# Eight of eleven routing pieces of the second batch behind the slots of the first expert phase, and no warm-up matmuls ahead of its first two phases

## What is computed

```python
h = tok(x, W, b);  h = concatenate([cls_tok, h], axis=1)
h = h + attn(layernorm(h))              # scores minus 0.2 x their 8 neighbours, softmax, values
# the part around the change, on x = layernorm(h), per token:
w_fk = topk_sparsify(softmax((x @ W_fk + b_fk) @ emb_fk_n.T), 4)   # 4 of 128 experts, first layer
w_rk = topk_sparsify(softmax((x @ W_rk + b_rk) @ emb_rk_n.T), 4)   # 4 of 128 experts, second layer
hid  = sum_n w_fk[n] * (x @ f_know[n])   # 192 -> 128
out  = h + sum_n w_rk[n] * (hid @ r_know[n])   # 128 -> 192
```

## Time and profile before

| What | Value |
|---|---|
| Time, median of 3 runs | 823.0 us (820.96 to 825.43) |
| Time of the profiled execution | 822.98 us |
| Its span | 821.3 us |
| Mean granted clock of TensorE | 0.856 |
| TensorE, matmuls | 615.0 us (75%) |
| VectorE | 378.1 us (46%) |
| ScalarE | 359.1 us (44%) |
| GpSimd | 400.6 us (49%) |
| Bytes moved by DMA | 147.13 MB, mean 179 GB/s |

### The profile page before, as it was taken

How to read it: one execution, slowest core, us unless ns; L and a number is a source line. 1 busy time by engine, 2 the same in 40 slices (tenths; PEclk the granted TensorE clock), 3 DMA queues, 4 the chain that set the end, 5 groups by cost and what they waited for, 6 DMA issues and landing times.

```text
span 821.3 us, 14397 instructions
## 1 busy us (share of the span) xinstructions
PE 615.0 (75%) x4572; PEld 517.9 (63%) x4572; DVE 378.1 (46%) x1337; ACT 359.1 (44%) x760; POOL 400.6 (49%) x397
## 2 busy tenths in 40 slices
PE   6798998989998874575999999988199804998000
PEld 5586876868787653343999889877187603676000
DVE  2846678879597999966930011110011110231132
ACT  4337285574757362234344434433047502576000
POOL 2433260523423056620773067774477773771674
PEclk9789999999998997655999999989599956999555
DMA  5253729476440675891577567799989724897432
GB/s 137 58 194 121 257 76 356 133 281 233 147 199 21 119 162 129 220 219 30 168 219 184 134 183 200 208 316 342 259 224 255 201 65 109 243 269 199 129 96 69
DMA packets 139574, 147.13 MB, mean 179 GB/s; under 512 B 12025, under 2 KB 123042, under 8 KB 139490
## 3 DMA queue, kind: packets, MB, share of 16 engines
q1 hardware_dynamic: 126114, 118.63, 50.2%
q0 software_dynamic: 13376, 27.41, 11.5%
HBM read 73.50 MB, written 72.50 MB: 178 GB/s over the span
## 4 chain that ended last, share of the span: by engine, by line
PE 41%; DVE 20%; POOL 11%; issue 11%; ACT 8%; DMA 6%; SPq 2%; POOLq 0%; DVEq 0%; ACTq 0%
PE bank L1231 19%; POOL gat L772 7%; PE bank L921 5%; PE bank L1219 5%; ACT qk_pad L1337 4%; POOL mid_dram L780 4%; DVE pick L2004 3%; PE bank L968 3%; DMA gat<-wide_dram,slots 2%; DMA wide_dram<-os_pair 2%; PE bank L1240 2%; DVE smax L1778 2%; PE bank L906 1%; DVE probs L1781 1%; PE bank L985 1%
## 5 line engine op out<-in xcount | busy, mean ns | idle before, releaser
L1231 PE MATMUL bank<-matrices,xsT 96*64 (+1 forms) x1632 | 224.6, 295 | 0.0
L1231 PEld LDWEIGHTS bank<-matrices,xsT 96*64 96x64 f32 (+1 forms) x1632 | 192.8, 139 | 23.1 <-issue 5.7
L772 POOL DMA_INDIRECT gat<-wide_dram,slots x152 | 145.9, 960 | 124.4 <-SPq L606 77.0
L757 POOL DMA_INDIRECT wide_dram<-x2b,slots x76 | 75.0, 987 | 84.0 <-issue 42.6
L2052 DVE TENSOR_SCALAR acc<-gat,wts 128x128 f32<-128x128 f32 x19 | 6.1, 319 | 231.7 <-DMA gat<-wide_dram,slots 231.7
L714 POOL TENSOR_TENSOR qk_sum<-qk_pad 64x888 f32<-64x888 f32 x16 | 26.8, 1676 | 155.5 <-ACT qk_pad L1337 139.0
L1548 ACT ACTIVATE os_pair<-bank 64x384 f32<-64x384 f32 x136 | 58.5, 478 | 72.3 <-DMA wide_dram<-os_pair 36.9
L780 POOL DMA_INDIRECT mid_dram<-comb,slots x76 | 74.0, 974 | 27.8 <-issue 21.6
L1561 ACT ACTIVATE xsT<-bank 96x512 f32<-96x512 f32 (+1 forms) x136 | 59.6, 487 | 58.2 <-PE bank L1219 56.8
L1542 ACT ACTIVATE os_pair<-bank 64x512 f32<-64x512 f32 x68 | 40.3, 592 | 85.3 <-PE bank L1231 79.1
L921 PE MATMUL bank<-tok_wT,pixT 128*128 128x192 f32 x384 | 70.6, 345 | 1.3 <-ACT pixT L1314 1.3
(11 more groups left out here) (196 smaller groups left out, 914.9 us busy)
## 6 DMA issues: line engine op xcount, KB each, us to landing
wide_dram<-zeros SPq DMA_DIRECT2D x6, 3328.0 KB, 14.0
mid_dram<-zeros SPq DMA_DIRECT2D x8, 1664.0 KB, 17.7
xs<-wide_dram SPq DMA_DIRECT2D x68, 192.0 KB, 3.1
wide_dram<-os_pair SPq DMA_DIRECT2D x68, 192.0 KB, 3.7
matrices<-in_L_ffn_f_know SPq DMA_DIRECT2D x8, 1536.0 KB, 15.2
matrices<-in_L_ffn_r_know SPq DMA_DIRECT2D x8, 1536.0 KB, 12.2
wide_dram<-os_pair SPq DMA_DIRECT2D x68, 128.0 KB, 2.8
xs<-mid_dram SPq DMA_DIRECT2D x68, 128.0 KB, 4.0
```

What stands on the lines that cost most here:

```text
L757: pool.indirect_dma_start(wide_dram[b], bass.IndirectOffsetOnAxis(ap=slots[:, t, e:e + 1], axis=0), x2b[:, t - BATCHES[b][0], :], None)\
L772: pool.indirect_dma_start(gat[i][:, e, :], None, wide_dram[b], bass.IndirectOffsetOnAxis(ap=slots[:, t, k:k + 1], axis=0))\
L1231: last = pe.matmul(out_bank[0:W, n * width:(n + 1) * width], xsT[r][0:kp, c:c + W], matrices[0:kp, bass.ds(starts[(r * SB + k) * 2 + half] ...
```

## The change

The pieces are renamed from `ahead` to `piece`. Pieces 0 to 2 stay ahead of phase 0; piece 3 + 4s + r follows, in phase 0, the products of slot r of step s on TensorE and its results on ScalarE, so that pieces 3 to 10 stand behind the eight slots of steps 0 and 1. `WARM` is 0 for phases 0 and 1 (24 and 20 before) and stays 24 and 16 for phases 2 and 3. Matrix chunk 7 is issued behind the loads of phase 0's first four slots instead of ahead of the waits for plan and scatters. The loads of the second layer's matrices are as they were: five in phase 1, six at its end. The whole diff:

```diff
--- before.py
+++ after.py
@@ -59,9 +59,9 @@
 DEPTH = (4, 3)
 PAIRS = RING // 2
 VALUE_BANK = (4, 6, 2, 5)
-WARM = (24, 20, 24, 16)
+WARM = (0, 0, 24, 16)
 SHARED = 3
-ROUTED = 11
+PIECES, ROUTED = 11, 3
 MIN_STEPS = -(-min(hi - lo for lo, hi in BATCHES) * ROWS * TOPK // (OWNED * W))
 assert MIN_STEPS > SHARED
 Y_BANK = (2, 4, 5, 6)
@@ -521,7 +521,7 @@
 
             sp.wait_ge(res_used, GROUPS + 1)
             sp.wait_ge(stored, 64 * GROUPS + 1)
-            load_f(range(6, EXPERTS // CHUNK))
+            load_f(range(6, 7))
 
             def load_rows(ph, s, r):
                 layer, b = PHASES[ph]
@@ -617,6 +617,7 @@
             sp.wait_ge(scattered[0], 64 * BATCHES[0][1])
             for r in range(RING):
                 load_rows(0, 0, r)
+            load_f(range(7, 8))
             expert_rows(0, rows_of_second)
             expert_end(0)
             sp.dma_start(x2b[:, 0:BATCHES[0][1], :], h2_tiles[:, 0:BATCHES[0][1], :]).then_inc(h2x_loaded, 16)
@@ -1166,7 +1167,7 @@
                 pe.matmul(bank[7][:, c:c + 256], x2T[t % 3][:, 0, :], r_mat[:, 0, :], start=True, stop=False)
                 return pe.matmul(bank[7][:, c:c + 256], x2T[t % 3][0:DH, 1, :], r_mat[0:DH, 1, :], start=False, stop=True)
 
-            def ahead(k):
+            def piece(k):
 
                 if k == 0:
                     ranks_after(t0)
@@ -1199,7 +1200,7 @@
                     plan(1, k - 8)
 
             for k in range(ROUTED):
-                ahead(k)
+                piece(k)
 
             def experts(ph):
 
@@ -1267,6 +1268,9 @@
                                     transposed(s + 1, r)
                         for r in (2 * q, 2 * q + 1):
                             products(s, r, starts)
+                            k = ROUTED + s * RING + r
+                            if ph == 0 and k < PIECES:
+                                piece(k)
 
                 each_step(pe, used, 0, step)
 
```

## The result

The changed kernel takes 813.5 us as the median of 4 runs (809.98 to 816.06), against 823.7 us for the kernel before on the same chip: ratio 0.9876, 95% interval 0.9827 to 0.9925, so 10 us (6 to 14) faster. Every ratio and interval in this document is taken from the undisturbed ("fast") runs alone, so where some runs of the kernel before were slow it is not the quotient of the two medians beside it. The profiled execution took 809.98 us, the quickest of the four; its span is 13.1 us under that of before. `<-issue` in the views is idle time in which the engine waited for nothing that the trace shows.

What follows compares the result with a forecast made beforehand. Bound: the chain of waits through TensorE's phases 0 and 1 to the batch 1 gathers at 581.01 us. Phase 1 starts 16.9 us earlier, less 3.0 us of low clock: 822.98 - 13.9 = 809 us, range 804 to 818 us.

Steps and rivals of the forecast that it cites:

- scatters as the next bound: Between phases 0 and 1: the last batch 1 scatter, at 454.6 us, sets the start of phase 1.
- 9 us of hand-over: Last batch 1 scatter to ScalarE's first copy of phase 1: 9.2 us, as between phases 2 and 3.
- first transposes of phase 0: TensorE's start of phase 0: 369.5 us in place of 395.60 us, including 2.34 us of value reads.
- low clock in phase 0, lost: Start of phase 0 without warm-up: 6.0 us of work at half speed, 3.0 us lost.
- waits up to piece 10: Phase 0: waits that the eight pieces add, 1.0 us in all, between nothing and 4 us.
- piece 10 ends: Last piece in phase 0: 369.5 + 25.9 of work + 1.0 of waits + 3.0 of low clock = 399.4 us.
- ScalarE's first copy of phase 1: Start of phase 1: 463.8 us in place of 480.67 us, 16.9 us earlier.
- what phase 1 takes more than before: Phase 1: 3.0 us lost to low clock at its start, after TensorE has been idle.
- The rival row: From 364.0 to 371.8 us TensorE is busy yet the clock stays at 0.50; cited for the late-clock rival.
- two clock rivals: Phase 0: clock up only near 391 us, 817 us, chance 0.10; or low until piece 10, 832 us, chance 0.08.
- chunk's cover: Phase 0: moved matrix chunk costs nothing, needed 28 us later at step 3, or over 30 us later by GpSimd.
- the gain is lost in phase 1: Rival: phase 1's matrix loads cost their stall again, 4 us idle and 3 us of clock; 816 us, chance 0.07.

Runs made afterwards that it cites:

- chunk7_back: Changed kernel with matrix chunk 7 issued ahead of the first rows of phase 0 again; 817.34 us, ratio 0.9947.
- moved_warm_kept: Changed kernel with the warm-ups of phases 0 and 1 kept (24 and 20 matmuls); 814.21 us, ratio 0.9907.
- warm_removed_only: Kernel before with only the warm-ups of phases 0 and 1 removed; 815.54 us, ratio 0.9897.
- half_scatter: Changed kernel with two of the four row scatters of each batch 1 tile left out; 799.34 us, ratio 0.97.
- after_again: The changed kernel itself, run again on a slower chip; 1030.06 us against 1050.66 us for the kernel before, ratio 0.9796.

## Why the prediction was right

The time lies in its range (804 to 818 us), with the sign as forecast, and the mechanism held up to and with the start of phase 1: pieces into phase 0, scatters as the next bound, 9 us of hand-over. 809 us was 4.5 us low against the median, and a gain of 13.9 us was forecast where 10.2 us were measured. By its steps, against the profiled execution:

| Step | Forecast | Measured |
|---|---|---|
| first transposes of phase 0 | 369.5 | 368.94 |
| wait for their rows | 0 | 0 |
| low clock in phase 0, lost | 3.0 us | 0.3 us |
| waits up to piece 10 | 1.0 us | 1.6 us |
| piece 10 ends | 399.4 | 397.27 |
| batch 1 scatters, first and last | 404.9, 454.6 | 402.76, 452.35 |
| TensorE ends phase 0 | 453.9 | 453.18 |
| ScalarE's first copy of phase 1 | 463.8 | 461.74 |
| what phase 1 takes more than before | 3.0 us | 7.3 us |
| gathers of batch 1 | 567.1 | 569.38 |

**The start.** The pieces end 1.7 us later than in the execution before (the last logits start at 366.16 where they did at 364.43 us), but the value reads' 2.34 us cost nothing: the transposes follow the rank matmuls at 368.94 us without a gap. My reading is that they ran beside matmuls that were already queued, where in the earlier trace rows TensorE had waited just before them; that is not shown, and between phases 0 and 1 the reads do leave 2.9 us idle behind 7.2 us of products. Two errors of the step so cancel, by luck: the 1.7 us are what executions differ by.

**The clock in phase 0.** It rose at 369.5 us, behind a stretch in which TensorE had worked without a gap from 365.7 us, through logits and ranks. The forecast had it at 374 to 377 us, and so it came in chunk7_back (377.3 us), behind a wait; that it came 5 us or more sooner here, worth 2.7 us, is luck. The rival row, 7.8 us of the same work at 0.50, is no rule either: with the same instructions the clock rose at 367.3, 369.5, 370.1 and 371.0 us in the traces of moved_warm_kept, the changed kernel, warm_removed_only and half_scatter, 3.4 to 3.8 us after TensorE began to work without a gap. The two clock rivals (817 and 832 us) are out. The rule of the Trainium skill that spoke for the slower one (TensorE: Matmul & The Clock Gate, "A second HAM failure mode: psum-queue depth-cycling") is not borne out here: through all eight pieces, with waits of 0.4 to 1.25 us, the granted clock stays 1.00 from 371 us on. Behind the 1.51 us wait of phase 1 it did fall, at 471.9 us.

**The waits.** 1.25 us for ScalarE, whose first copy starts at 370.76 us, 0.8 us behind its last exponential, and 0.39 us for the rows of step 1, which queued behind the moved chunk and took 9.4 us to land: 1.6 us. The 0.77 us of issue at 397.27 us lie behind piece 10 and delay only what TensorE does next. 25.9 + 0.3 + 1.6 = 27.8 us stand against the measured 28.3 us from 368.94 to 397.27 us; the slots and pieces themselves took 0.5 us more than forecast. The chunk's cover, 30 us by my count, was of the wrong user: what the chunk delays is the rows of step 1, which are needed 10 us later.

**The hand-over.** From the last scatter's start to ScalarE's first copy 9.4 us passed, where the phase 2 to 3 row gave 9.2 us. Half_scatter shows that the scatters set it.

**Phase 1** is the term of the sum that was mis-sized, 7.3 us for 3.0. From its first copy to the gathers it took 107.6 us, 100.3 before. At its start TensorE runs 10.7 us at low clock; from the first copy to the transposes of step 1 it takes 9.8 us in place of 5.5, of which 1.5 are the wait for rows behind the `x2b` reload. That wait and the work around it bring the clock down a second time (473.34 us: 4.64 us for 3.64), and the next pair takes 6.4 in place of 4.7 us. At the end of the phase the last stores take 2.0 us more: 8.4 us from the last product (553.76 us, 7.20 us long) to the gathers, 6.4 us before, counted from this line:

```profile
...
567.37 7.20 PE L1231 MATMUL bank<-matrices,xsT 96*64 x64
...
```

What makes the stores slower is open. 4.3 + 1.7 + 2.0 us is 8.0 us; the stalls on the matrix loads change by +1.1 and -1.1 us and the clock behind them gives 0.7 back. I had priced one low-clock start and no wait for rows behind it. The rival "the gain is lost in phase 1" (7 us, 0.07) named another mechanism, the matrix loads, and that one did not come: their stalls change by nothing in sum. That 4.3 us were lost all the same is not to its credit. The version with the warm-ups kept shows that the low clock at the start was not by itself the term to price: without it the phase took as long, since the wait for rows and the low clock behind it grew. The wait at 470 us comes from the order of SyncE's queue: the rows of step 1 are issued only behind the landing of phase 0's last stores, and right behind the reload. TensorE asks for them 3.8 us after their issue (466.29 to 470.04 us), and 1.3 us after it in moved_warm_kept, where it waits 3.42 us; where it asks 5.8 and 6.8 us after it, in warm_removed_only and half_scatter, it does not wait. That the reload is what makes them land in 5.2 us, where such loads take 2.9 us in the median, is argued and not shown. A rival is untested: GpSimd's gathers of batch 0 start in the same microsecond (466.17 us).

**The rest.** That the profiled run is within 1.0 us of 809 us is in part luck: the gathers of batch 1 came 2.3 us later than forecast, and the part behind them, which the change does not touch and the forecast left as it was, took 1.4 us less than before (240.6 against 242.0 us). The median is 3.5 us above the profiled run. The four runs spread over 6 us, with granted clocks of 0.847 to 0.856; where that time lies is open, since only one left a trace.

## What to carry to other kernels

Work taken off a path uncovers what had slack beside it: here 26.7 us came off the start of phase 0, but the scatters that the same edit delayed had 30 us of slack, and they ended up setting the next start. Before adding two gains (here the removed warm-ups, 8 us alone, and the moved pieces, 9 us with the warm-ups kept), ask which wait both end in. A warm-up in front of a phase costs its length and is worth only the low-clock time it replaces: little if TensorE has worked up to that point (0.3 us here). In a wait it costs nothing, but it gained nothing either here, since the next rows were hardly there sooner.

## What the runs showed of the hardware

Value reads that left TensorE idle for 2.34 us in front of phase 0 left no gap in the changed kernel, where they follow rank matmuls directly; in front of phase 1 they left 2.9 us idle in the kernel before, in warm_removed_only and in half_scatter. The clock came back 3.4 to 3.8 us into unbroken transposes, logits and rank matmuls in four traces, 5.0 to 6.2 us into transposes and products in others (372.3 to 377.3 us in chunk7_back, 387.8 to 394.0 us in warm_removed_only), and not within 7.8 us of the former work in the trace of before. It fell 1.7 and 1.9 us into the idle stretches ahead of phase 1 (changed kernel, half_scatter), and not in one of 2.4 us (moved_warm_kept). And a chip can run the same program 28% slower (1051 against 823 us) with VectorE, ScalarE and GpSimd busy for the same time (377, 358 and 400 us): 19% of after_again's chain is issue and 13% another core or an unknown queue, where the changed kernel on the first chip had 11% of issue.
